# Sending the first key stacks from ScalarE's queue, and the second block's stacks ahead of the maxima, in an attention and mixture-of-experts kernel

## The reference

```python
q = proj(Wq, bq); k = proj(Wk, bk); v = proj(Wv, bv)        # y = x @ W.T + b, 16 heads of 8
out = chunked_attention(q, k, v, CHUNK, scale)              # causal softmax(q k^T * scale) v
x = _layernorm(x + out @ Wo.T + bo)
logits = x @ router_w.T;  top_idx = argmax(logits);  score = sigmoid(max(logits))
moe_out = onehot(top_idx) * (silu(xs @ gate) * (xs @ up)) @ down      # xs = x * score
x = _layernorm(x + moe_out + silu(x @ s_gate) * (x @ s_up) @ s_down)
```

## Time and profile before

| what | value |
|---|---|
| median of three runs | 597.0 us |
| profiled execution, its own time | 598.1 us |
| its span in the trace | 596.4 us |
| PE busy | 531.0 us (89%) |
| VectorE (DVE) busy | 452.0 us (76%) |
| ScalarE (ACT) busy | 363.7 us (61%) |
| GpSimd (POOL) busy | 142.6 us (24%) |
| DMA, mean rate | 38 GB/s |
| granted TensorE clock, mean | 0.961 |

### The profile page before, as it was taken

How to read it: one execution, slowest core, us unless ns; L and a number is a source line. 1 busy time by engine, 2 the same in 40 slices (tenths; PEclk the granted TensorE clock), 3 DMA queues, 4 the chain that set the end, 5 groups by cost and what they waited for, 6 DMA issues and landing times.

```text
span 596.4 us, 12259 instructions
## 1 busy us (share of the span) xinstructions
PE 531.0 (89%) x4393; PEld 202.1 (34%) x4393; DVE 452.0 (76%) x765; ACT 363.7 (61%) x805; POOL 142.6 (24%) x268
## 2 busy tenths in 40 slices
PE   5478898899999999999999999999998999998980
PEld 3233233333323333222222223223224225664460
DVE  4796999999888888886888789779824425767683
ACT  3015666566777666777777776776797884331450
POOL 4623320312203021020101002002013157214744
PEclk9657999999999999999999999999999999999995
DMA  6341000240010511000010010000001012211233
GB/s 155 101 114 51 2 2 29 72 117 28 2 28 2 154 34 29 2 6 24 1 28 2 1 28 2 2 2 2 1 1 36 20 34 56 45 50 40 48 66 92
DMA packets 28875, 22.49 MB, mean 38 GB/s; under 512 B 3528, under 2 KB 28048, under 8 KB 28816
## 3 DMA queue, kind: packets, MB, share of 16 engines
q1 hardware_dynamic: 26848, 18.43, 10.9%
q0 software_dynamic: 1536, 3.15, 3.0%
q10 hardware_dynamic: 432, 0.13, 0.1%
HBM read 8.00 MB, written 4.06 MB: 20 GB/s over the span
## 4 chain that ended last, share of the span: by engine, by line
PE 61%; DVE 20%; ACT 6%; issue 6%; POOL 5%; DMA 2%; POOLq 0%; SPq 0%; DVEq 0%; ACTq 0%
PE ring_ps L1280 20%; PE out_ps L1300 19%; DVE part_max L982 13%; PE score_ps L1244 7%; ACT probs L857 4%; PE score_ps L1390 3%; PE ring_ps L1407 1%; PE score_ps L1280 1%; PE ring_ps L1211 1%; PE ring_ps L1310 1%; PE score_ps L1251 1%; POOL k_stack L797 1%; PE score_ps L1342 1%; POOL k_stack L687 1%; POOL qk_parts L784 1%
## 5 line engine op out<-in xcount | busy, mean ns | idle before, releaser
L982 DVE TENSOR_REDUCE part_max<-score_ps 128x2 f32<-128x1024 f32 (+3 forms) x320 | 324.6, 1060 | 56.7 <-PE score_ps L1244 29.5
L857 ACT ACTIVATE probs<-ring_ps 128x512 f32<-128x512 f32 (+3 forms) x603 | 287.4, 531 | 114.7 <-PE ring_ps L1280 111.8
L1280 PE MATMUL ring_ps<-q_stack,k_stack 64*128 64x512 bf16 (+3 forms) x1206 | 203.3, 351 | 10.7 <-ACT probs L857 7.8
L1300 PE MATMUL out_ps<-probs,v_aug 128*32 128x512 f32 (+3 forms) x1280 | 151.4, 544 | 4.4 <-POOL probs L717 4.1
L1244 PE MATMUL score_ps<-k_stack,q_stack 64*128 64x512 bf16 (+3 forms) x640 | 110.5, 362 | 21.0 <-DVE part_max L982 14.3
L1280 PEld LDWEIGHTS ring_ps<-q_stack,k_stack 64*128 64x128 bf16 x1206 | 53.2, 94 | 133.7 <-ACT probs L857 109.3
L717 POOL TENSOR_SCALAR_AFFINE_SELECT probs<-probs 128x512 f32<-128x512 f32 x64 | 40.7, 636 | 183.8 <-ACT probs L857 183.6
L1244 PEld LDWEIGHTS score_ps<-k_stack,q_stack 64*128 64x128 bf16 x640 | 31.7, 95 | 91.6 <-DVE part_max L982 62.9
L1300 PEld LDWEIGHTS out_ps<-probs,v_aug 128*32 128x32 f32 x1280 | 25.5, 108 | 49.9 <-ACT probs L857 24.3
L784 POOL DMA_INDIRECT qk_parts<-xs_dram,q_stack x30 | 30.6, 1019 | 26.3 <-DVE q_stack L1109 18.5
L1251 PE MATMUL score_ps<-mask_wide,ident_wide 64*128 64x128 bf16 (+1 forms) x512 | 35.8, 222 | 0.0
(11 more groups left out here) (177 smaller groups left out, 405.5 us busy)
## 6 DMA issues: line engine op xcount, KB each, us to landing
q_stack<-qk_parts SPq DMA_DIRECT2D x36, 128.0 KB, 2.5
k_stack<-qk_parts SPq DMA_DIRECT2D x36, 128.0 KB, 2.4
sorted_dram<-q_stack SPq DMA_DIRECT2D x30, 64.0 KB, 1.5
x_sb<-in_L_attn_x_dram SPq DMA_DIRECT2D x4, 256.0 KB, 4.4
w_gu<-n_L_ffn_expert_gate_dram SPq DMA_DIRECT2D x8, 128.0 KB, 2.1
w_gu<-in_L_ffn_expert_up_dram SPq DMA_DIRECT2D x8, 128.0 KB, 2.2
wd<-n_L_ffn_expert_down_dram SPq DMA_DIRECT2D x8, 128.0 KB, 2.3
xs_dram<-qk_f SPq DMA_DIRECT2D x4, 256.0 KB, 2.3
```

The source lines that it names most:

```text
L857: act.activation(probs[:, u % RING, 0:w], bank(("probs", u))[:, 0:w], ACT.Exp, scale=SCALE).then_inc(probs_ready, 1)
L982: dve.tensor_reduce(out=part_max[:, s % 2, t, 2 * hp:2 * hp + 2, c], in_=score_ps[:, m % 2, :, 0:w], axis=AX.X, op=ALU.max).then_inc(score ...
L1280: last = mm(bank(unit)[:, 0:w], k_stack[half, j // TPB, rows, hh, keys], q_stack[half, B % 2, rows, hh, skip:BLK], start=rows == MAIN, sto ...
L1300: last = mm(out_ps[at:at + 32, skip:BLK], v_aug[:, j, h * VC:h * VC + 32], probs[:, (4 * k + i) % RING, 0:w], start=j == 0, stop=j == TPB ...
```

## The change

`stack` takes the queue as an argument. SP's queue now sends the first block's query stacks alone, and behind them all of block 1's stacks, ahead of the loop over the plan and so ahead of every placement of maxima. The first block's key stacks are issued by ScalarE's queue, in the branch for `k_in` of block 0, behind `rT`.

```diff
+        def stack(queue, side, b, part):
...
+            if part == PARTS - 1:
+                queue.wait_ge(first_part_kept, 2 * b + side + 1)
+            else:
+                queue.wait_ge((q_split, k_split)[side], (PARTS - 1) * b + PARTS - 1 - part)
...
+            for p, product in enumerate(PRODUCTS):
+                if product[side] == part:
+                    queue.dma_start(to[p:P:HD, at, MAIN, :, :], parts).then_inc((q_stacked, k_stacked)[side][b], 16)
+            if part == 0:
+                queue.wait_ge((q_filled, k_filled)[side], (min(b, 1), b)[side] + 1)
+                queue.dma_start(to[0:P:HD, at, REST, :, :], parts).then_inc((q_lows_stacked, k_lows_stacked)[side][b], 16)
...
             def stack_block(b):
                 for part in reversed(range(PARTS)):
                     for side in range(2):
-                        stack(side, b, part)
+                        stack(sp, side, b, part)
...
-            stack_block(0)
+
+            for part in reversed(range(PARTS)):
+                stack(sp, 0, 0, part)
+            stack_block(1)
...
-                    if s == 0:
-                        stack_block(1)
...
                         act.activation(rT[:, :], score_ps[:, 1, 1, 0:E], ACT.Copy).then_inc(w_kept, 1)
+                        for part in reversed(range(PARTS)):
+                            stack(act, 1, 0, part)
```

More of the change, by code:

```diff
@@ L571, in last_quad @@
             return next(it[1:] for it in plan if it[0] == "values" and it[2:] == (B, g, TPB * (B + 1) - 1))
+        def stack(queue, side, b, part):
+            to = (q_stack, k_stack)[side]
+            at = b % 2 if side == 0 else b
+            parts = qk_parts[:, side, b % 2, part, :]
+            if part == PARTS - 1:
+                queue.wait_ge(first_part_kept, 2 * b + side + 1)
+            else:
+                queue.wait_ge((q_split, k_split)[side], (PARTS - 1) * b + PARTS - 1 - part)
+            if side == 0 and b >= 2:
+                queue.wait_ge(exp_in_ready, units_before[b - 1])
+            for p, product in enumerate(PRODUCTS):
[4 more added lines that the diff above has]
+                queue.dma_start(to[0:P:HD, at, REST, :, :], parts).then_inc((q_lows_stacked, k_lows_stacked)[side][b], 16)
         @block.sync
@@ L585, in _ @@
                              x_tiles[:, TPB * b:TPB * b + TPB, :]).then_inc(x_loaded[b], 16)
[L587 to L604, removed]
             def stack_block(b):
```

## The result

The changed kernel takes 602.83 us (median of 5 runs, 601.58 to 604.49) against 597.0 us before. The ratio is 1.0075 with a 95% interval of 1.0053 to 1.0098: slower by 3.2 to 5.9 us. The profiled execution after has a span of 602.8 us, against 596.4.

What follows compares the result with a forecast made beforehand. The bound was the chain from `xT`'s copy through GpSimd to the first maxima. 4.2 + 0.95 = 5.15 us, rounded to 5.2, on a 597.0 us median gave 602.2 us; range 599.6 to 604.5.

Steps and rivals of the forecast that it cites:

- The chain: Up to PE's turn of the first maxima: starts at ScalarE's copy of `xT`, 12.95 us; the key-stack wait lies beside it.
- ScalarE's nine issues, 4.2 us: ScalarE ahead of block 1's `xT`: issues of 5.8 us in all make the copy 4.2 us late, bounds 2.6 to 4.8.
- PE's product at the lower clock, 0.95 us: Block 1's q product: 5 us of PE idle time lowers the clock, so ScalarE starts 2.08 us behind it, not 1.13.
- GpSimd carries 5.15 us: GpSimd's memset L685 to the first maxima: the whole 5.15 us arrives at PE's turn, and nothing later takes it up.
- First scores and block 1's stacks, 0 us each: Earlier key stacks gain nothing at VectorE's first reduction, about 26.3; block 1's stacks ahead of the maxima neither cost nor gain.
- the landing: Block 0's stacks on both queues: landing 2.5 us from issue, over by 20 us.
- The cover up to PE's first score: Slack between the key stacks' landing and PE's first score: some 3 us.
- The estimate of 280 GB/s for the DMA engines: All 16 engines with two queues move some 280 GB/s; used as the upper bound, ScalarE 4.8 us late.
- Rival B, issues that take turns: Issues on ScalarE and SP alternate, 18 ending at 20.94: 605.9 us, half of it some 604; chance 0.12.

Runs made afterwards that it cites:

- e1: Changed kernel with block 1's stacks put back behind the first placement of maxima, only ScalarE's nine issues kept: 601.77 us, ratio 1.0067 against the kernel before.
- e7: Kernel before with the nine key-stack issues on ScalarE, but behind block 1's first parts of q and k: ratio 0.9994 against the kernel before.
- e9: Kernel before with two of the nine key-stack issues on ScalarE, seven on SP with the REST issues last, GpSimd's fills not moved: ratio 1.0019 against the kernel before.
- e6: Kernel before with GpSimd's two memsets (blocks 2 and 3 of the key stacks) moved behind the first maxima: ratio 0.9964 against the kernel before.
- e4: Changed kernel with 32 unused transposes on PE while it waits for block 1's `xT`: ratio 1.0059 against the kernel before.
- e2: Kernel before with only block 1's stacks on SP moved ahead of the maxima: ratio 1.0005 against the kernel before.
- e10: Repeat: kernel before with two key-stack issues on ScalarE, SP's REST issues last, GpSimd's two fills behind the first maxima: 596.24 us, ratio 0.9965 against the kernel before.

## Why the prediction was right, step by step

*The chain.* Right. It was read that the chain starts at the copy of `xT` and that the wait for key stacks is not on it; `e1` and `e7` show the first, `e9` the second. What it left out is how near the other path was: before, PE waited only 0.18 us for GpSimd at the turn, and `e6` gained only 0.15 us there.

*ScalarE's nine issues, 4.2 us.* Measured 4.42 (12.95 to 17.37). Two errors nearly cancel, which is luck: the first issue began at 10.74, before `rT` had ended and not behind it, 0.6 us earlier than forecast, and the nine took 6.59 us (10.74 to 17.33) in place of 5.8. It is not simply SP's issuing beside them that made them longer: the issue at 12.97 took 0.62 us while SP issued, the one at 15.95 took 0.72 with SP's nine ended at 15.65.

*PE's product at the lower clock, 0.95 us.* Measured 2.06 against 1.11 in the chain; the clock fell in the window from 16 us, PE being idle since 12.64. `e4` shows that it is the idle time. That the size fits so well is luck in part: it was taken from the first block's product, behind which ScalarE started 2.08 us later at a granted clock of 1.00 (6 to 10 us in the profile of before), so slow for another reason than the granted clock.

*GpSimd carries 5.15 us.* Measured 5.38 at its memset and 5.40 at the turn. The rest of the kernel keeps it, as forecast, as far as the clock behind step 2 lets one see that.

*First scores and block 1's stacks, 0 us each.* Right: the first reduction was forecast near 26.3 and came at 26.34; `e2` shows the second. But the landing, put at 2.5 us from issue and over by 20, was not: ScalarE's eight issues from L588 took 3.3 to 6.1 us to land, and the last of them, issued at 15.95, landed near 21.9, against 22.1 for the same stack before. The cover up to PE's first score at 23.36 was so 1.5 us and not 3, and the second queue brought the keys some 0.3 us forward, whatever it held up.

*The estimate of 280 GB/s for the DMA engines.* Wrong, though nothing hung on it but an upper bound. The same stretch before and after (columns as in the earlier trace rows):

```profile
12.00:22.00 10.00, 3.75 (x21) 2.40 (x19) 8.01 (x20) 1.97 (x3) 1.63 (x1) 0.92 0.74 203
```

```profile
12.00:22.00 10.00, 4.52 (x12) 2.24 (x12) 3.85 (x10) 1.38 (x3) 0.00 (x0) 0.72 1.03 211
```

With both queues at work the changed kernel moved 256 and 247 GB/s in the first two microseconds of it, then 205 to 226 at a busy share of 1.11 to 1.14 up to 21 us, and 211 over all; one queue had moved 203 at 0.74. The busy share is no measure of what is left.

*Rival B, issues that take turns.* It falls: by turns each issue would have taken some 1.3 us, and the nine took 0.73 each with the steps between them. The Trainium skill's page "Perfetto Trace Analysis", section "DMA Instruction — HWDGE (DVE, Sync)", has the two sequencers lock a shared block; here the nine took 6.59 us, against 5.85 in `e7_act_late`, where ScalarE issued alone, so on average at most 0.08 us an issue can be that. The Trainium skill's page "DMA: Bandwidth & Descriptors", section "Issuing engines are not separate DMA queues", says that issuing from several engines only saves the sequencer's time; the 4% more bandwidth above agrees.

*The size.* The trace gives 5.4 us, the median 5.8, the two ratios of the changed kernel 4.5 and 4.2. The last two are lower than the sum. The slow start of PE seen in `e2_sp_half` and `e10` would explain it: it costs an execution of the kernel before some 2 us, and one of the changed kernel nothing, since that pays for the slow product anyway. I did not show this.

## What to carry to other kernels

A DMA issue on an engine's queue is work of that engine, in its program's order: cost it at the place where it stands, by what is queued behind it, and look for idle time there (1.62 us here held two issues, not nine). A long wait in the list is worth nothing while another path meets it at the same step; `e9` moved one path by 1.3 us for no gain, and with the other path moved too the kernel became faster, though in these executions the clock was higher as well. A second queue brings copies forward only as far as the DMA engines had room: here 4% more bandwidth. And an engine that is made to wait can come back slower: of the loss here 0.95 us was PE's clock after 5.48 us without work.

## What had not been expected of the hardware

- The DMA engines moved nearly as much for these copies with one queue issuing as with two: 203 GB/s from 12 to 22 us with SP alone, 211 with both. With two queues a copy waited longer behind its issue: 5.5 us to landing for ScalarE's nine (median), against 2.4 for the key stacks before.
- An issue on ScalarE's queue starts beside the activation ahead of it: 10.74 us, with `rT` from 10.88 to 11.06. The activation behind it waits until the last issue is done.
- PE's slow rate at the start of the program lasts differently long from one execution to the next: block 1's products took 1.95 us in the profile of before and 3.75 in those of `e2_sp_half` and `e10_two_on_act_again`, with a granted clock of 1.00 in the windows from 14 to 18 us of both, so these rows do not show what slowed it.
